# Expert dispatch by a slot table: token rows gathered into SBUF tiles in place of scattered into slots in memory

## The reference, cut to what matters

```python
h = h + attention(layernorm(h))
x = layernorm(h)                              # [1104, 256]
shared = gelu(x @ up_s) @ down_s              # one shared expert, 256 -> 1024 -> 256
probs = softmax(x @ router_w)                 # 8 routed experts
top_k_prob, top_k_idx = top_k(probs, 2)       # two experts per token
routed = sum over the 2 picks of prob * expert(x)
out = h + shared + routed + x
```

## Time and profile before

| | us |
|---|---|
| runs | 409.56, 410.15, 439.06 |
| median | 410.15 |
| span of the profiled execution, first to last instruction | 400.7 |
| median less span, the launch and end around it | 9.45 |
| busy: PE, DVE, ACT, POOL | 309.9, 229.3, 118.4, 239.3 |

### The profile page before, as it was taken

How to read it: one execution, slowest core, us unless ns; L and a number is a source line. 1 busy time by engine, 2 the same in 40 slices (tenths; PEclk the granted TensorE clock), 3 DMA queues, 4 the chain that set the end, 5 groups by cost and what they waited for, 6 DMA issues and landing times.

```text
span 400.7 us, 6810 instructions
## 1 busy us (share of the span) xinstructions
PE 309.9 (77%) x2019; PEld 277.8 (69%) x2020; DVE 229.3 (57%) x494; ACT 118.4 (30%) x239; POOL 239.3 (60%) x164
## 2 busy tenths in 40 slices
PE   1069574987689559998669999989999999999500
PEld 0057474777578349998548999979898989898500
DVE  4218888897868997855994254543565333333000
ACT  2136342251132222211032434334343434343000
POOL 2247553864815870578987077699978564565341
PEclk9999885996959788999698999999999999999955
DMA  8971139041142032232435205255342245344322
GB/s 219 318 180 28 44 108 288 2 131 50 35 133 90 11 110 110 74 133 88 168 127 171 95 13 165 84 166 188 118 144 106 41 56 76 46 49 51 40 26 26
DMA packets 22996, 41.17 MB, mean 103 GB/s; under 512 B 2623, under 2 KB 19457, under 8 KB 20673
## 3 DMA queue, kind: packets, MB, share of 16 engines
q0 software_dynamic: 7056, 24.46, 22.5%
q1 hardware_dynamic: 14480, 15.14, 13.6%
q10 hardware_dynamic: 1440, 1.33, 1.3%
HBM read 29.01 MB, written 11.90 MB: 102 GB/s over the span
## 4 chain that ended last, share of the span: by engine, by line
PE 41%; DVE 21%; DMA 21%; issue 7%; POOL 6%; POOLq 2%; ACT 1%; ACTq 0%; SPq 0%; DVEq 0%
DMA out_tokens<-y_all,dest 10%; PE ps L788 10%; PE ps L789 9%; PE ps L790 9%; DMA ring<-in_tok_w 5%; PE ps L654 5%; PE ps L838 5%; DVE hid L1137 4%; DMA h_after_attention<-h 3%; POOL ring L340 2%; DVE hid L1136 2%; POOLq L483 2%; DVE qk L1034 1%; DVE h L1072 1%; DMA h2f<-h_after_attention 1%
## 5 line engine op out<-in xcount | busy, mean ns | idle before, releaser
L340 POOL TENSOR_TENSOR ring<-stage,ring 128x2048 fp32r<-128x2048 f32 (+1 forms) x21 | 84.5, 4026 | 1.8
L486 POOL DMA_INDIRECT out_tokens<-y_all,dest x25 | 39.0, 1561 | 41.8 <-DMA out_tokens<-y_all,dest 30.7
L1305 DVE TENSOR_TENSOR hgT<-ps,hgT 128x512 fp32r<-128x512 f32 x50 | 32.2, 685 | 54.7 <-ACT hgT L644 54.7
L788 PE MATMUL ps<-ring,hgT 128*128 x200 | 57.9, 290 | 2.4 <-DVE y_all L1312 1.5
L789 PE MATMUL ps<-ring,hgT 128*128 x200 | 56.0, 280 | 0.0
L790 PE MATMUL ps<-ring,hgT 128*128 x200 | 55.9, 280 | 0.0
L339 POOL TENSOR_SCALAR ring<-stage 128x2048 fp32r<-128x2048 f32 (+1 forms) x21 | 36.6, 1742 | 23.4 <-PE ps L790 21.6
L636 ACT ACTIVATE hg<-ps 128x512 f32<-128x512 f32 x50 | 29.9, 599 | 51.9 <-PE ps L790 51.9
L788 PE MATMUL ps<-ring,xgT 128*128 x100 | 42.8, 428 | 2.1 <-POOLq L345 1.0
L789 PE MATMUL ps<-ring,xgT 128*128 x100 | 40.4, 404 | 0.0
L790 PE MATMUL ps<-ring,xgT 128*128 x100 | 40.2, 402 | 0.0
(11 more groups left out here) (167 smaller groups left out, 665.8 us busy)
## 6 DMA issues: line engine op xcount, KB each, us to landing
stage<-in_w_up POOLq DMA_DIRECT2D x9, 1024.0 KB, 5.2
stage<-in_w_dn POOLq DMA_DIRECT2D x9, 1024.0 KB, 5.3
slots<-gact SPq DMA_DIRECT2D x1, 3262.5 KB, 13.4
xg<-slots SPq DMA_DIRECT2D x25, 130.5 KB, 2.1
xp<-in_patches SPq DMA_DIRECT2D x6, 288.0 KB, 7.6
h_after_attention<-h SPq DMA_DIRECT2D x4, 276.0 KB
h2f<-h_after_attention SPq DMA_DIRECT2D x8, 128.0 KB, 2.0
ring<-in_tok_w ACTq DMA_DIRECT2D x1, 768.0 KB, 21.7
```

What stands on the lines that cost most here:

```text
L340: return nc.gpsimd.tensor_tensor(lo, stage[:, part, c0:c1], hi.bitcast(F32), ALU.subtract)
L486: pool.indirect_dma_start(out, bass.IndirectOffsetOnAxis(ap=dest[:, t:t + 1].bitcast(U32), axis=0), y_all[:, t, :], None, compute_op=ALU.a ...
L788: nc.tensor.matmul(o, a[0], b[0], start=n == 0, stop=False)
L1305: v.tensor_tensor(hgT[:, c, 1, 4 * half:4 * half + 4, :], ps[:, turned_bank + half, :].rearrange("p (k t) -> p k t", k=4), hgT[:, c, 0, 4 ...
```

## The change

The slots in memory, their fill, the 18 scatters and the five numbers beside each row go. The normalized rows are written by SP, in token order and with plain DMAs, to a memory tensor `normalized_tokens`, followed by 128 rows of zeros. DVE makes from the slot numbers, for every (token, pick), a one-hot row of the tile it is in, weighted with the token number and with the gate (`told`), and a one-hot row of its place in the tile (`in_lane`). 18 small matmuls contract these over the tokens: the result is a table of 128 places by 25 tiles with the token number (`dest`) and the gate (`gate`) of every slot. With `dest` as indices POOL gathers each tile's rows from memory into `xy_all`, which later takes the results as well; SP copies a tile from there to `xg`. The first 7 tiles have a place that is free at once; the other 18 use the bytes of the shared expert's input and wait for its last up product (`s_up`). The buffer `hid` becomes a ring of five slices in place of two halves of eight. On POOL, the first half of expert 2 is now prepared ahead of the dispatch and the second half between gathers 7 and 8. The token number and gate are no longer picked out tile by tile. The five short operations that make the table of the output waits (L1292 to L1297) move from behind the third chunk of the shared expert to ahead of it.

```diff
+HB = 5
+EARLY_ROWS = TILES - 18
...
-    slots_d = nc.dram_tensor("slots", [TILES * P, XW], F32).ap()
+    xn_d = nc.dram_tensor("normalized_tokens", [T + P, D], F32).ap()
...
         hT_n = sb("hT_n", [P, 2, KD, TPAD], F32R, shared, "right")
-        hid = sb("hid", [P, 2, KF, SN], F32R, shared, "right")
+        sb("gap", [P, EARLY_ROWS, D], F32, shared, "right")
+        hid = sb("hid", [P, HB, 2, SN], F32R, shared, "right")
         shared.close()
+        xy_all = sb("xy_all", [P, TILES, D], side="right")
...
-            sp.dma_start(slots_d.rearrange("(t p) w -> p t w", p=P),
-                         gact[:, 0:1, 0:XW].to_broadcast([P, TILES, XW])).then_inc(slots_init, 16)
-
-            sp.dma_start(out[T:T + P, :], gact[:, 0, 0:D]).then_inc(slots_init, 16)
+            sp.dma_start(xn_d[T:T + P, :], gact[:, 0, 0:D]).then_inc(xn_out, 16)
+            sp.dma_start(out[T:T + P, :], gact[:, 0, 0:D]).then_inc(trash_in, 16)
+
+            def keep_rows(tiles):
+                for i in tiles:
+                    sp.wait_ge(f_normed, i + 1)
+                    sp.dma_start(xn_d[P * i:P * i + ROWS[i], :], hx[0:ROWS[i], i, :]).then_inc(xn_out, 16)
...
+                keep_rows(flat_tiles_after(g))
+            keep_rows(flat_tiles_after(NG))
...
-            sp.wait_ge(slots_out, 16 * 2 * NT)
-            for t in range(2):
-                sp.dma_start(xg[:, t, :], slots_d[P * t:P * (t + 1), :]).then_inc(x_in[t], 16)
...
+            for t in range(TILES):
+                sp.wait_ge(rows_in[t % 2], 16 * (t // 2 + 1))
+                if t >= 2:
+                    sp.wait_ge(x_tr, t - 1)
+                sp.dma_start(xg[:, t % 2, :], xy_all[:, t, :]).then_inc(x_in[t % 2], 16)
...
-            pool.wait_ge(slots_init, 32)
-            pool.wait_ge(r_slots, 1)
-            for i in range(NT):
-                for k in range(2):
+            def gather_rows(t0, t1):
+                for t in range(t0, t1):
+                    if t >= 2:
+                        pool.wait_ge(rows_in[t % 2], 16 * (t // 2))
                     pool.indirect_dma_start(
-                        slots_d, bass.IndirectOffsetOnAxis(ap=slot_i[0:ROWS[i], k, i:i + 1].bitcast(U32), axis=0),
-                        hx[0:ROWS[i], i, :], None).then_inc(slots_out, 16)
-            for x in range(2, NX):
+                        xy_all[:, t, :], None, xn_d,
+                        bass.IndirectOffsetOnAxis(ap=dest[:, t:t + 1].bitcast(U32), axis=0)).then_inc(rows_in[t % 2], 16)
+
+            prepare_half(2, 0)
+            pool.wait_ge(r_table, 1)
+            pool.wait_ge(xn_out, 16 * (NT + 1))
+            gather_rows(0, EARLY_ROWS)
+            prepare_half(2, 1)
+            pool.wait_ge(s_up, NSG * KF)
+            gather_rows(EARLY_ROWS, TILES)
+            for x in range(3, NX):
                 for part in range(2):
                     prepare_half(x, part)
...
-            last.then_inc(r_prefix, 1)
-            shared_steps(11, NSG * KF)
+            nc.tensor.matmul(ps[:, 6, LANES:LANES + P], ones, upper, start=True, stop=True).then_inc(r_prefix, 1)
+            shared_steps(11, TABLE_AT)
+
+            te.wait_ge(r_told, 1)
+            for n in range(2 * NT):
+                r = ROWS[n % NT]
+                last = nc.tensor.matmul(ps[:, 6, TABLE:TABLE + 2 * TILES], in_lane[0:r, n, :],
+                                        told[0:r, n, :, :].rearrange("p a t -> p (a t)"),
+                                        start=n == 0, stop=n == 2 * NT - 1)
+            last.then_inc(r_table_mm, 1)
+            shared_steps(TABLE_AT, NSG * KF)
...
-                    if q >= 1:
-                        dve.wait_ge(s_down, n - KF + 1)
-                    link(v.tensor_copy(hid[:, 0, f, :], gact[:, n % 2, :]))
-                    v.tensor_tensor(hid[:, 1, f, :], gact[:, n % 2, :], hid[:, 0, f, :].bitcast(F32),
+                    if n >= HB:
+                        dve.wait_ge(s_down, n - HB + 1)
+                    link(v.tensor_copy(hid[:, n % HB, 0, :], gact[:, n % 2, :]))
+                    v.tensor_tensor(hid[:, n % HB, 1, :], gact[:, n % 2, :], hid[:, n % HB, 0, :].bitcast(F32),
                                     ALU.subtract).then_inc(s_lo, 1)
...
-            for k in range(2):
-                v.tensor_copy(hx[:, :, C_GATE + k], rsm[:, 3 + k, :])
-                last = v.tensor_scalar(hx[:, :, C_EXP + k], rsm[:, 5 + k, :], -1.0, float(NE), ALU.mult, ALU.add)
-            last.then_inc(r_mask, 1)
...
+            v.tensor_scalar(lanes[:, :], ps[:, 6, LANES:LANES + P], -float(P), None, ALU.add)
             link(v.tensor_copy(rtab[:, 0, :], ps[:, 6, NE * NT:NE * (NT + 1)]))
...
-                link(v.tensor_reduce(rsm[:, k, :], n3(rout[:, 6 + k, :]), AX.X, ALU.add))
-                link(v.tensor_copy(slot_i[:, k, :], rsm[:, k, :]))
-            v.tensor_copy(tend_int[:, :], rtab[0:1, 2, :]).then_inc(r_slots, 1)
+                last = v.tensor_reduce(slot[:, NT * k:NT * (k + 1)], n3(rout[:, 6 + k, :]), AX.X, ALU.add)
+            link(last)
+            link(v.tensor_copy(tend_int[:, :], rtab[0:1, 2, :]))
+
+
+            TO = 2 * NT
+            link(v.tensor_tensor(above[:, :, :], slot[:, :].unsqueeze(2).to_broadcast([P, TO, TILES]),
+                                 tile_from[:, :].unsqueeze(1).to_broadcast([P, TO, TILES]), ALU.is_ge))
+            link(v.tensor_reduce(turn_count[:, :], above[:, :, :], AX.X, ALU.add))
+            link(v.scalar_tensor_tensor(out=lane[:, :], in0=turn_count[:, :], scalar=-float(P), in1=slot[:, :],
+                                        op0=ALU.mult, op1=ALU.add))
+            v.tensor_copy(in_tile[:, :, TILES - 1:], above[:, :, TILES - 1:])
+            v.tensor_tensor(in_tile[:, :, 0:TILES - 1], above[:, :, 0:TILES - 1], above[:, :, 1:TILES], ALU.subtract)
+            link(v.tensor_tensor(mark[:, :].rearrange("p (k n) -> p k n", k=2),
+                                 token[:, :].unsqueeze(1).to_broadcast([P, 2, NT]),
+                                 lane[:, :].rearrange("p (k n) -> p k n", k=2), ALU.subtract))
+            v.tensor_tensor(told[:, :, 0, :], in_tile[:, :, :], mark[:, :].unsqueeze(2).to_broadcast([P, TO, TILES]), ALU.mult)
+            v.tensor_tensor(told[:, :, 1, :], in_tile[:, :, :],
+                            rsm[:, 3:5, :].rearrange("p k n -> p (k n)").unsqueeze(2).to_broadcast([P, TO, TILES]), ALU.mult)
+            v.tensor_tensor(in_lane[:, :, :], lanes[:, :].unsqueeze(1).to_broadcast([P, TO, P]),
+                            lane[:, :].unsqueeze(2).to_broadcast([P, TO, P]), ALU.is_equal).then_inc(r_told, 1)
             shared_parts(KF + 2, KF + 4)
...
-            shared_parts(KF + 4, 2 * KF + 2)
-            shared_end(SG, 2 * SG)
-            def x_low(s, c, first=False):
-
-                dve.wait_ge(x_in[c], 8 * s + (32 - 8 * c))
-                et = etab[:, bass.ds(s + 2, 1)]
-                if not (first and s < 0):
-                    dve.wait_ge(x_meta, s + 1)
-                v.scalar_tensor_tensor(out=junk[:, c, :], in0=xg[:, c, C_EXP:C_EXP + 2], scalar=et,
-                                       in1=xg[:, c, C_GATE:C_GATE + 2], op0=ALU.is_equal, op1=ALU.mult,
-                                       accum_out=gate[:, bass.ds(s + 2, 1)])
-                v.tensor_copy(dest[:, bass.ds(s + 2, 1)], xg[:, c, C_TOK:C_TOK + 1]).then_inc(x_meta, 1)
+            def x_low(s, c):
+
                 dve.wait_ge(x_hi, s + 3)
                 v.tensor_tensor(xgT[:, c, 1, :, :], ps[:, 4, 0:KD * P].rearrange("p (k t) -> p k t", k=KD),
                                 xgT[:, c, 0, :, :].bitcast(F32), ALU.subtract).then_inc(x_lo, 1)
 
-            shared_parts(2 * KF + 2, 3 * KF)
-            for s in (-2, -1):
-                x_low(s, s % 2, first=True)
-            shared_end(2 * SG, NT)
-
-
+            shared_parts(KF + 4, TABLE_AT)
+            dve.wait_ge(r_table_mm, 1)
+            v.tensor_copy(gate[:, :], ps[:, 6, TABLE + TILES:TABLE + 2 * TILES])
+            v.tensor_scalar(dest[:, :], ps[:, 6, TABLE:TABLE + TILES], small[:, S_SPARE:S_SPARE + 1], None,
+                            ALU.add).then_inc(r_table, 1)
```

More of the change, by code:

```diff
@@ L104, in fusion_layer @@
         tend_int = sb("tend_int", [1, NE], I32)
-        slot_i = sb("slot_i", [P, 2, NT], I32)
+        slot = sb("slot", [P, 2 * NT])
+        lane = sb("lane", [P, 2 * NT])
+        mark = sb("mark", [P, 2 * NT])
+        turn_count = sb("turn_count", [P, 2 * NT])
+        lanes = sb("lanes", [P, P])
+        tile_from = sb("tile_from", [P, TILES])
+        token = sb("token", [P, NT])
+        gate = sb("gate", [P, TILES])
+        dest = sb("dest", [P, TILES], I32)
         rw = sb("rw", [P, KD, NE])
@@ L156, in fusion_layer @@
         ring = sb("ring", [P, RING, 2, EW], F32R)
-        xg = sb("xg", [P, 2, XW])
+        table = ExitStack()
+        above = sb("above", [P, 2 * NT, TILES], where=table)
+        in_tile = sb("in_tile", [P, 2 * NT, TILES], where=table)
```

(24 more changed lines are left out.)

57 lines of the change are left out of this document (25 added, 32 removed).

## The result

| | runs | median us | lowest to highest |
|---|---|---|---|
| before, beside it | 4 | 409.86 | 407.54 to 439.06 |
| after | 4 | 414.82 | 413.51 to 416.29 |

Ratio 1.018, 95% interval 1.013 to 1.024. Executions more than 1.5% above the fastest of their kernel (439.06 here, 1650.8 in experiment 9) count in the medians and not in the ratios. The median is 0.7 us from the forecast of 415.5. The profiled execution took 416.29 us with a span of 414.4: 1.9 us lie around it, where the prediction had put 9.45 around the span before. Experiments 1 and 2 show that this matters.

A forecast was written before the change was run, and what follows sets the result against it. Bound: the start of the output DMA queue, set by POOL's list. POOL is 5.6 us late at expert 3 (PE 1.2), the queue's 78 us unchanged: 410.15 + 5.4 = 415.5 us; own range 411 to 420, whole range 406 to 424.

The forecast's parts named there:

- D: PE's delay in the routed phase: first matmul 8.5 late, less 4.45 and 2.9, +1.2 us.
- G: Time at which POOL begins to prepare expert 3, after the gathers: forecast 227.7, POOL 5.6 us late.
- even point: Start of POOL's preparation of expert 3 beyond which POOL's lateness moves the end: 222.1.
- rival one: Late gathers run at the output DMAs' pitch, 1.86 us, landing 3.4: +13.0, 423 us; chance 0.24.
- the early edits: Slot fill removed and row writes by SP before the dispatch: zero effect, at most +1 us.
- Router: POOL's early half of expert 2 holds DVE at L1209; mask at 159.1 in place of 155.15: +1.7 us for PE.
- Table on DVE: New table operations take 5.9 us, `told` ready at 171.0; PE idles 5.1 us, slower clock costs +1.4.
- Second half of expert 2: After seven gathers, POOL's half holds DVE at slice 18 until 197.4; PE's down product waits: +2.9 us.
- Late gathers: 18 gathers after the last up product, from 201.6, at a pitch of 1.45 us, 26.1 us in all.
- Hand-over: Shared expert to first routed matmul takes about 3.0 us instead of 9.6; first matmul at 206.9, 8.5 late.
- Two: POOL and PE stay even: early half does not hold the router, pitch 1.34; -2.4 us, 407.7; chance 0.14.
- three: Table is off PE's path, DVE's 5.9 us absorbed by PE's lead: -7.4 us, 402.7; chance 0.10.

The follow-up runs named there:

- experiment 9: Kernel before with expert 2's first half ahead of the scatters and eight output DMAs between weight splits, run on another chip: 384.52 us, ratio 0.957.
- Experiments 1 and 2: Both kernels again, unchanged: before 400.05, 409.54 and 399.98 us on three chips; after 415.36 and 414.86 on the last two, ratios 1.017 and 1.037.
- experiment 3: Kernel after with four gathers in flight in place of two: 407.95 us, ratio 1.019 to a before of 400.05.
- experiment 4: Kernel after with the early half of expert 2 moved back behind the seven early gathers: 416.87 us, ratio 1.039 to before.
- group 3's after: Kernel after, unchanged, on the third chip: 414.86 us beside a before of 399.98, ratio 1.037.
- Experiment 7: Kernel before with the table's DVE operations and 36 small matmuls added and their result unused: 419.9 us, ratio 1.029.
- group 2's chip: Chip of the second set of runs sharing one before: before 409.54 us, after 415.36, ratio 1.017.
- experiment 8: Kernel before with expert 2's first half ahead of the scatters and eight output DMAs moved between weight splits: 390.82 us, ratio 0.955.
- groups 1 and 3: Sets of runs on two other chips, each sharing one before: before 400.05 and 399.98 us; after only in the latter, 414.86.

## Why the prediction was right in its median, and where it was not

**The path and the rule: right.** POOL's list sets the start of the output queue, and the end moves by the larger of D and G - 222.1. Measured in the trace after: G = 234.8, so 12.7; the last output DMA moved by 406.65 - 393.89 = 12.8. With each group's own before (expert 5 at 252.51 and 252.06, so an even point of 221.5 and 221.1) G is late by 3.1 in experiment 3, 14.3 in experiment 4 and 10.5 in group 3's after, and the queue starts 3.6, 14.6 and 10.9 later. Experiment 7 shows the other branch, D. The 78 us of the queue stayed. PE's waits for POOL came at experts 3 (4.03 us) and 5 (1.42 at 280.49), but not at 4.

**The start of the sum: wrong by 7.4 us.** I took 9.45 us as what lies around the span and added the shift to 410.15. Every later profiled execution has about 2.0 there. The trace was of an execution of some 402.7 us; none of the runs listed beside it took that. 402.7 + 12.8 = 415.5: the shift was 7.4 us too small, the start 7.4 too large, and they cancelled. That is luck: with the measured G my own sum would have read 410.15 + 12.7 = 422.9, rival one's time. (The sum also took 5.4 where its own G gives 5.6.) On the chips where before takes 400, the same forecast of the shift would have been 9.5 us short (14.9 measured, 5.4 forecast).

**Why before differs between chips: partly open.** Shown: kernels with the 18 scatters can have a stretch of 9 to 10 us in which DVE (and ACT) stand still beside them, on group 2's chip in both traces; in the one pair that can be compared (experiments 8 and 9) the end is later by its length. It is not in the four traces of such kernels in groups 1 and 3, nor in the first profile, and in none of the seven traces of kernels with gathers, two of them on that chip. 409.5 less 400 is of the size of such a stretch, and it would explain why the change cost only 5 us on that chip. But no trace of the unchanged kernel at 409.5 was obtained, and what the engines lack in the stretch is not in the profile. PE also has a gap of 2.69 us there in experiment 7 with nothing waited for. Late instructions are a candidate that was not tested: from 165 to 200 us the two queues of kind instruction moved one packet each in experiment 8 and two and one in experiment 9, which settles nothing.

**The sizes, in the trace after.** The late gathers start at 206.20 and not 201.6, and G is 4.6 later by that and 2.5 by the pitch. Single executions are compared here, and they differ before the router already: the shared expert's first matmul is at 113.01 in the trace before and at 111.10 in this one, between 107.9 and 111.1 in the seven traces with gathers and between 108.5 and 113.4 in the seven with scatters. Differences of a microsecond or two between starts are therefore not safe, and whether the early edits gave anything is not shown.
- Router: the mask at 159.97 and not 159.1. DVE was held by the early half as said, but in a cast of a slice (4.74 us for 0.35), not in L1209's successor. That a hold falls on two-input operations was my rule, and too narrow. The Trainium skill, SBUF — State Buffer, "Who interferes with whom", says that casts and `tensor_scalar` can take the shared port pair too; the casts of 4.74 and 2.29 us (after and experiment 4) and L1325 agree. The trace before had shown it too: a cast of 2.63 us at 187.22. The cost that I took for the hold, 1.7, is what experiment 4 gave back, as far as single executions tell.
- Table on DVE: 171.71 and not 171.0; PE's stall 4.58 for 5.1; clock 0.57 for four microseconds, as taken. Table on PE: 4.11 for 3.9. `dest` at 181.9 for 180.5.
- Early gathers: 1.52 us each for 1.45.
- Second half of expert 2: it does not fall on slice 18 but on the output table's operations, L1322 and L1325, 6.8 us for the two where the same operations took 0.23 and 0.17 in the trace before. I had counted the table as 1.2 us ahead of the slice. PE resumes at 199.88 and not 197.4, after a stall of 3.99 where I had 2.9. **That stall pulls the clock down again** (0.57 from 200 to 204), which the sum left out though it had counted it for the first stall: the late gathers start 6.3 us after PE resumes and not 4.2. Of these 2.1, 4 x 0.43 = 1.7 are the clock.
- Late gathers: 1.63 us each and not 1.45, past the 1.60 at which I had said that rival one decides and outside the 1.34 to 1.60 that I had named as a sign of being wrong. G, 234.8, is past its 230.3 as well. By my own signs this term failed. Two pitches less the 0.3 to issue give a landing of 2.95 us where I had estimated 2.6; over 18 gathers that is 28.6 us in place of 26.1. Yet a gather does not land later than a scatter: the median from issue to landing is 2.8 us for gathers (group 3's after, experiment 3) and 2.7 to 2.8 for scatters (before in groups 1 and 3). The scatters waited for no landing; the gathers do, and that puts it into the pitch.
- Hand-over: first routed product at 211.27, 12.9 late; first result tile 225.4 against 219.3, so D = +6.1 and 6.8 us were given back, where I had 7.4. D was wrong (1.2) because the 12.9 was (8.5); it did not decide.

**The rivals.** One was half right: its mechanism, the landing in the pitch, is what passed the forecast, but at 1.63 and not 1.86; the measured G is within 0.3 of its 235.1 only because the start is 4.6 later as well. Two and three fell: the early half did hold DVE, and the table is on PE's path.

## What to carry to other kernels

Ask which queue sets the end, and what of the removed work stood in a time when that queue's engine owed nothing: 18 scatters in idle time were replaced by gathers behind the last moment at which their buffers came free, on the engine that is on the critical path. Let a gather wait for the one four before it and not two, and put waits for landings next to work of the same engine: moving eight output DMAs gave most of 4.5%, about what the choice between scatter and gather cost at most. Their places were chosen for one routing; another input would need others. And compare a profile's span with its own execution's time before adding a shift to a median, and count starts from an event that the change cannot reach.

## What the runs showed of the hardware that was not expected

- The same program takes 400 us on two chips and 409.5 on a third (19, 13 and 17 runs), with medians of after at 415 on two of these.
- DVE without work for 9.14 and 10.39 us beside a stream of scatters, with no wait in the profile that names what it lacked; the kernel with the 9.14 had none on another chip.
- A one-partition operation of 25 numbers took 4.39 us beside a 4.56 us operation of POOL.
- A stall of 4.0 us of PE costs about 1.7 more: the granted clock is 0.57 in the next four microseconds (0.63 in group 3's execution of after), and 1.00 after.
- With two gathers of 128 KB in flight the pitch is 1.52 to 1.63 us, with four 1.25, which is POOL's own issue and the 0.30 behind it.
